# Where the lower halves of the normalised input are subtracted: on VectorE between two list stages, or on GpSimd beside the count table

## What is computed

```
h = jnp.maximum(_layernorm(x, axis=-1), 0.0)      # the "normalised input"
x = x + gnn0(h, src, dst, ...)                    # pooled = segment_sum(h[col], row)
h = jnp.maximum(_layernorm(x, axis=-1), 0.0)
x = x + gnn1(h, src, dst, ...)                    # and so on, four times
```

## Time and profile before

| | us |
|---|---|
| median of three runs | 3275.98 |
| span of the profiled execution, first to last instruction | 3240.8 |
| what lies around the span (median less span) | 35.2 |
| first block, lists and normalised input | about 0 to 104 |
| second block, count table | about 104 to 417, its table builds 103.9 to 399 |

### The profile page before, as it was taken

The page is one execution under the profiler, slowest core; times in us unless marked ns, Lnnn a source line. Parts: engine busy times, 40 slices in busy tenths (PEclk is TensorE's granted clock), DMA queues, the critical chain, the costliest instruction groups (busy, mean ns, idle before and its releaser), DMA issues. The chain is left out here.

```text
span 3240.8 us, 44117 instructions
## 1 busy us (share of the span) xinstructions
PE 2943.5 (91%) x18657; PEld 1740.9 (54%) x18657; DVE 1047.2 (32%) x1860; ACT 729.8 (23%) x1173; POOL 1114.7 (34%) x1012
## 2 busy tenths in 40 slices
PE   1799969997899869999999999999899877999998
PEld 1688835553444335555555555554355664555554
DVE  5899922223200261211111111113311483222122
ACT  4799912223100230000000000001100383011000
POOL 5000013330000004562562663664167101553564
PEclk6899979998999979999999999999899987999999
DMA  7133599994466226666665665664566213665665
GB/s 260 50 129 129 163 244 173 164 170 89 120 147 146 44 66 206 178 171 169 177 175 165 182 178 163 173 173 121 146 181 179 78 54 101 176 180 161 171 170 156
DMA packets 768367, 492.61 MB, mean 152 GB/s; under 512 B 362500, under 2 KB 749836, under 8 KB 767568
## 3 DMA queue, kind: packets, MB, share of 16 engines
q1 hardware_dynamic: 705362, 395.76, 50.5%
q0 software_dynamic: 30112, 62.69, 6.6%
q10 hardware_dynamic: 32702, 31.44, 3.1%
HBM read 334.89 MB, written 76.82 MB: 127 GB/s over the span
## 5 line engine op out<-in xcount | busy, mean ns | idle before, releaser
L2159 PE MATMUL acc<-tbuf,hs 128*128 128x448 fp8e4 x8232 | 1602.0, 354 | 20.0 <-PEq L1242 8.8
L2136 POOL DMA_INDIRECT grow<-hrows,glist x882 | 940.6, 1066 | 791.9 <-PE acc L2183 388.3
L2159 PEld LDWEIGHTS acc<-tbuf,hs 128*128 128x128 f16 x8232 | 801.2, 98 | 762.9 <-issue 52.5
L2298 DVE TENSOR_TENSOR edge_loc<-iota,gdl 128x768 f16<-128x768 bf16 x147 | 140.6, 971 | 743.9 <-PE acc L2183 714.4
L731 PE MATMUL quad<-K,S 128*128 128x196 bf16 x1568 | 278.0, 250 | 17.6 <-DVE K L655 17.6
L1627 PE MATMUL acc<-tbuf,hs 128*128 128x512 fp8e4 (+1 forms) x1300 | 279.6, 369 | 14.9 <-DMA tbuf<-table 14.9
L711 ACT ACTIVATE stage<-quad 128x784 fp8e4<-128x784 f32 x392 | 287.4, 838 | 11.6 <-PE quad L731 5.8
L735 PE MATMUL deg<-K,S 128*128 128x196 bf16 x1568 | 276.8, 248 | 0.0
L1500 PE MATMUL acc<-tbuf,hs 128*128 128x512 fp8e4 (+1 forms) x1300 | 267.4, 369 | 0.7 <-issue 0.7
L2267 ACT ACTIVATE H<-B,vectors 128x448 f32<-128x448 f32 (+2 forms) x56 | 37.4, 668 | 820.3 <-DVE B L2338 820.3
L1500 PEld LDWEIGHTS acc<-tbuf,hs 128*128 128x128 f16 x1300 | 123.6, 98 | 144.4 <-issue 4.3
(11 more groups left out here) (301 smaller groups left out, 2008.5 us busy)
## 6 DMA issues: line engine op xcount, KB each, us to landing
tbuf<-table SPq DMA_DIRECT2D x294, 448.0 KB, 3.6
tbuf<-table SPq DMA_DIRECT2D x294, 336.0 KB, 3.2
table<-stage SPq DMA_DIRECT2D x6, 5488.0 KB, 19.4
grow<-hrows,glist POOLq DMA_INDIRECT x882
hrows<-hs SPq DMA_DIRECT2D x28, 448.0 KB, 4.4
feat<-in_edge_attr_dram ACTq DMA_DIRECT2D x27, 448.0 KB, 6.6
C<-factors ACTq DMA_DIRECT2D x2, 3136.0 KB, 12.5
table<-stage SPq DMA_DIRECT2D x2, 2744.0 KB, 12.2
```

The source lines that it names most:

```text
L2136: g.indirect_dma_start(out=grow[:, n % 2, t, :], out_offset=None, in_=k.hrows[l % 2], in_offset=bass.IndirectOffsetOnAxis(k.glist[:, i // ...
L2159: mm = T.matmul(acc(s, h), rows[l % 2][:, g * US + r, part, :], counts[:, (r - lo) * STRIP + h * HALF:(r - lo) * STRIP + (h + 1) * HALF], ...
L2298: V.tensor_tensor(hot[:, n % 2, :, :], k.iota[:, 0:P].unsqueeze(1).to_broadcast([P, GH, P]), k.gdl[:, i // GU, i % GU * GH:(i % GU + 1) * ...
```

## The change

`rests` and its semaphore go from VectorE's program of the first block. In the second block GpSimd, after its memsets, multiplies the four pieces of xn by 2^12 in place (four one-input instructions) and then subtracts the upper halves (four two-input instructions, each behind a semaphore of the multiplication of its piece). To live that long, `xn` becomes `k.xn`, a buffer of the whole program, which afterwards serves as `k.B`; two small tiles of `layer_norm` become local to it.

```diff
@@ first_stage
-        xn = sb("xn", [P, NL, D], F32)
+        xn = k.xn[:, :].rearrange("p (n f) -> p n f", f=D)
...
-                def rests(i):
-                    a, b = XQ[i]
-                    dve.wait_ge(hi_ok.h, hi_ok.at(i + 1))
-                    V.scalar_tensor_tensor(k.hs[:, a:b, 1, :], xn[:, a:b, :], 2.0 ** LN_SCALE, k.hs[:, a:b, 0, :],
-                                           ALU.mult, ALU.subtract).then_inc(lo_ok.h, 1)
...
                 windows(0)
-                for i in range(4):
-                    rests(i)
                 windows(1)
@@ build_tables, the program of GpSimd
                 nc.gpsimd.memset(empty[:, :], 0.0).then_inc(set_ok.h, 1)
+                for i, (a, b) in enumerate(XQ):
+                    nc.gpsimd.tensor_scalar(k.xn[:, a * D:b * D], k.xn[:, a * D:b * D], 2.0 ** LN_SCALE, None, ALU.mult
+                                            ).then_inc(scaled.h, 1)
+                for i, (a, b) in enumerate(XQ):
+                    pool.wait_ge(scaled.h, scaled.at(i + 1))
+                    nc.gpsimd.tensor_tensor(k.hs[:, a:b, 1, :], k.xn[:, a * D:b * D].rearrange("p (n f) -> p n f", f=D),
+                                            k.hs[:, a:b, 0, :], ALU.subtract)
@@ layer_norm
-    with nc.Block() as block:
+    with (nc.sbuf_tensor(f"rstd{k.next()}", [WCH, NW, CH], F32) as rstd,
+          nc.sbuf_tensor(f"halfway{k.next()}", [WCH, NW, CH], BF16) as halfway, nc.Block() as block):
@@ program, network
-        k.middle = sb("middle", [NCH, 2, CH], BF16)
-        k.rstd = sb("rstd", [NCH, 2, CH], F32)
+        k.xn = sb("xn", [P, NL * D], F32)
-        k.B, k.C = (big(n) for n in "BC")
+        k.B, k.C = k.xn[:, 0:NP], big("C")
```

More of the change, by code:

```diff
@@ L248, in first_stage @@
         stat_ok, std_ok, inv_ok, y_ok = k.sem("stat_ok"), k.sem("std_ok"), k.sem("inv_ok"), k.sem("y_ok")
-        hi_ok, lo_ok, y_out = k.sem("n_hi"), k.sem("n_lo"), k.sem("y_out")
+        hi_ok, y_out = k.sem("n_hi"), k.sem("y_out")
         e_in, e_pads, e_out = k.sem("e_in"), k.sem("e_pads"), k.sem("e_out")
@@ L583, in first_stage @@
     k.retire(x_in0=16, x_in1=16, x_in2=16, x_in3=32, x_pad=1, x_T=NGRP, x_copied=NGRP, stat_ok=4, std_ok=4, inv_ok=4,
-             y_ok=NL, n_hi=4, n_lo=4, y_out=80, e_in=96, e_pads=2, e_out=32, iotas=3, w_rows=1, firsts_T=2, rows_ok=1,
+             y_ok=NL, n_hi=4, y_out=80, e_in=96, e_pads=2, e_out=32, iotas=3, w_rows=1, firsts_T=2, rows_ok=1,
              offs_ok=NWG, w_count=NWG, chunk_in=16, pair_ok=2, spill_out=32, edge_ok=1, judged=1, seen_ok=3,
@@ L615, in build_tables @@
         stored = [k.sem("stored0"), k.sem("stored1")]
-        turn_sp = k.sem("b_turn_sp")
+        turn_sp, scaled = k.sem("b_turn_sp"), k.sem("b_scaled")
         deg_out, deg_T, deg_ok = k.sem("deg_out"), k.sem("deg_T"), k.sem("deg_ok")
@@ L749, in build_tables @@
     k.retire(hots=NHALF * NBATCH, batch_used=NHALF * NBATCH, filled=NHALF * NQUAD, moved_q=NHALF * NQUAD, stored0=80,
-             stored1=48, b_turn_sp=NU + 1, deg_out=16, deg_T=1, deg_ok=2, b_set=2, empty_out=32, b_judge=4, n_out=1, b_gather=7)
+             stored1=48, b_turn_sp=NU + 1, deg_out=16, deg_T=1, deg_ok=2, b_set=2, empty_out=32, b_judge=4, n_out=1, b_gather=7,
+             b_scaled=4)
 BOUNDS = ("rows", "z0", "z1", "z2", "z3", "first")
@@ L1011, in _ @@
                 dve.wait_ge(rooted.h, rooted.at(w + 1))
-                root, hi = k.rstd[0:WCH, w, :], k.parts[0:WCH, w, :]
+                root, hi = rstd[0:WCH, w, :], k.parts[0:WCH, w, :]
                 V.reciprocal(root, root).then_inc(inverse.h, 1)
@@ L1018, in _ @@
                 dve.wait_ge(middle.h, middle.at(w + 1))
-                V.tensor_tensor(k.parts[64:64 + WCH, w, :], root, k.middle[0:WCH, w, :], ALU.subtract
+                V.tensor_tensor(k.parts[64:64 + WCH, w, :], root, halfway[0:WCH, w, :], ALU.subtract
                                 ).then_inc(inverse.h, 1)
@@ L1037, in root @@
                 act.wait_ge(var.h, var.at((w + 1) * WCH))
-                A.activation(k.rstd[0:WCH, w, :], k.bank[2 + w][0:WCH, 0:CH], ACT.Sqrt, bias=k.eps[0:WCH, 0:1]
+                A.activation(rstd[0:WCH, w, :], k.bank[2 + w][0:WCH, 0:CH], ACT.Sqrt, bias=k.eps[0:WCH, 0:1]
                              ).then_inc(rooted.h, 1)
@@ L1048, in split @@
                 act.wait_ge(inverse.h, inverse.at(4 * w + 3))
-                A.activation(k.middle[0:WCH, w, :], k.rstd[0:WCH, w, :], ACT.Copy).then_inc(middle.h, 1)
+                A.activation(halfway[0:WCH, w, :], rstd[0:WCH, w, :], ACT.Copy).then_inc(middle.h, 1)
                 act.wait_ge(middle.h, middle.at(w + 1))
-                A.activation(k.parts[32:32 + WCH, w, :], k.middle[0:WCH, w, :], ACT.Copy).then_inc(moved.h, 1)
+                A.activation(k.parts[32:32 + WCH, w, :], halfway[0:WCH, w, :], ACT.Copy).then_inc(moved.h, 1)
             split(0)
```

## The result

| | median us (runs) | ratio to before, 95% interval |
|---|---|---|
| before | 3264.37 (22) | |
| changed | 3277.43 (22) | 1.0039 (1.0028 to 1.0049), +12.7 us |

A forecast was written before the change was run, and what follows sets the result against it. VectorE bounds the first block's end; in the count table VectorE, ScalarE and TensorE are within 2% of each other. -6.94 gained plus 17.2 lost gives +10.3 us on the median 3275.98, so 3286.3, range 3263 to 3300.

The forecast's parts named there:

- The gain: First block: removing the four subtractions from VectorE's path saves 6.94 us in full.
- strict alternation: Second block's start: eight GpSimd instructions and VectorE's builds take turns over 29.6 us; VectorE loses 18.5 us.
- The fifth batch's S: Sign in the count table: this build starts some 29 us into the second block, before at 12.8.
- The subtractions: Second block: four two-input GpSimd instructions, 6400 elements at 2.06 ns, take 13.2 us and hold VectorE's builds.
- The multiplications: Second block: four one-input GpSimd instructions, priced by the affine select, take 6.4 us and hold VectorE's builds.
- the upper bound: Second block: GpSimd's one-input instructions take at most 13.2 us, the two-input price.
- The other estimate in the prediction: Second block: 1.03 cycles per element on GpSimd makes the multiplications about 5.5 us and the sum +9.4.
- The wait for TensorE: Count table's third and fourth batch: half of VectorE's 2.61 us of waiting, 1.3 us, is saved.
- That VectorE keeps the path: Rival, second block: GpSimd waits or the two don't exclude each other; only the 6.94 us are left, 3269.0; chance 0.14.
- That only the subtractions count: Rival, second block: multiplications, reading one tile, don't hold VectorE; +4.4 us, 3280.4; chance 0.08.
- The clock staying low: Rival, count table: TensorE stays at 1.2 GHz; +227 us for the rest of the table, 3513; chance 0.03.
- That the gain falls short: Rival, first block: second list half moves less than 6.94 us; at worst nothing gained, +17.2, 3293.2; chance 0.03.

The follow-up runs named there:

- The fills alone: Changed kernel with GpSimd only filling the lower halves with zero in the second block, multiplications and subtractions left out; ratio to before 0.9977.

## Why the prediction was right, and where it was off

**The gain.** -6.94 us, forecast and measured. The fills alone (0.9977) confirm it as time.

**The mechanism.** VectorE is held while GpSimd reads, each GpSimd instruction gets its turn although VectorE always has a build ready, and nothing downstream hides it. All three are in the rows of the changed kernel: eight long builds, eight instructions, +23.2 us of stage. The order of the turns was not the forecast's strict alternation. Of the eleven builds from 97.24 to 130.71 three K builds passed at 1.57 us, all beside the multiplications, and GpSimd ended 38.0 us into the block, where 29.6 were forecast. The fifth batch's S started 22.3 us into the block, not 29; that sign failed, and the sum did not hang on it.

**The subtractions.** The forecast had 13.2 - 0.6 = 12.6 us of hold; 12.0 were measured. The price of 2.06 ns per element from L1671 and L1673 was right within 3% (2.01 alone).

**The multiplications.** This is the term that was mis-sized. The forecast took the affine select's 0.99 ns per element, the nearest row by kind, and had 6.4 - 0.6 = 5.8 us of hold; 12.2 were measured. Alone the instruction takes 2.67 ns per element. Two errors stand against each other in it: the length was 17.0 us for the four alone, not 6.4, and 4.8 of these did not hold VectorE, where the forecast gave 0.14 for each instruction, 0.6 in all. So the upper bound, 13.2 us by the two-input price, held for the hold, partly by luck, and fell short for the length. The other estimate in the prediction, about 5.5 us and a sum of +9.4, missed by more: that price per element is not this instruction's.

**The wait for TensorE.** 1.3 us were taken as saved, 0.65 were. The clock rose during the alternation and was at 1.2 GHz again at its end, so neither of the two pictures behind that half was quite right.

**Sum.** 12.2 + 12.0 - 0.65 - 6.94 = +16.7 by the holds, +15.5 by the marker, +12.7 by the ratio, for the +10.3 of the forecast. Its bounds, +8 to +18, hold all three.

**The time.** 3277.43 us lie inside the 3263 to 3300 that were given, but that is weak evidence. The cost was larger than forecast, and yet the time came out 9 us under the forecast's 3286.3, because the forecast stood on the first three runs of before, whose median lay 12 us above that of all 22. Here two errors met by luck. The range also held the times of three rivals (3269, 3280 and 3293). What bears the mechanism out is the rows and the experiments. The 1% that the prediction named as the least a measurement can tell was too much: with 22 runs of each kernel the interval is 0.2% wide.

**The rivals.** That VectorE keeps the path is excluded by the eight long builds. That only the subtractions count is excluded by the run with the multiplications alone. The clock staying low is excluded: it was at 2.4 GHz from 142 on. That the gain falls short is excluded, since the second list half started without a wait, 6.94 us sooner.

**What stays open.** Why a multiplication of one tile takes GpSimd longer than a subtraction of two. And why VectorE is free again about 1 us before the multiplication ends, and hardly before the subtraction does: the hold is 3.0 of 4.1 us at 1536 elements, and 2.9 of 3.1 for the subtraction. At 6400 elements it is 15.8 of 17.0, but there GpSimd's instruction had begun 0.7 us before the build that it held, so the two lengths don't compare. That it is reading, and not some other trait of these instructions, that holds VectorE rests on the fills against the two kinds that read; no run took a GpSimd instruction that computes without reading this memory.

## What to carry to other kernels

Moving elementwise work from VectorE to an idle GpSimd does not take it off VectorE when the instructions beside it read two tiles from SBUF: VectorE then loses GpSimd's time, here 24 us for the 7 it saved. Before giving work to another engine, look for a stretch in which the first one waits for something unrelated; here 12.2 us of it stood at the end of the same block. And an operation without a row of its own should be bounded by the dearest relative on that engine, not priced by the one that looks most like it; here even the dearest, 13.2 us, fell short of the 17.0 that the multiplications took alone.

## What the hardware showed that was not expected

- GpSimd's float32 multiplication by a constant, in place, on 1536 elements took 4105 ns, its two-input subtraction of the same size 3086 ns.
- VectorE was free again about 1 us before such a multiplication ended (1.0 us in the run with the multiplications alone, 0.9 in the run with the eight instructions behind the builds).
- VectorE instructions of next to no work were held too: L681, one element per partition with two inputs, for 2.0 us, and L698, seven elements with one input, for 3.8 us.
- TensorE's clock stood at 2.4 GHz from 106 to 112 us, in which TensorE worked for 2.65 us. It was at 1.2 GHz from 127 to 137, after 0.06 us of work between 122 and 127, and VectorE's wait for TensorE behind it was 1.96 us.
